# Second attention's front token-major: Newton roots on GpSimd, and VectorE's row operations in other slots

## The reference, cut to what matters

```
q_c = (xh W_DQ) W_UQ            # per head: 512 tokens x 16 features
q_c_norm = q_c * rsqrt(mean(q_c^2) + EPS) * q_norm_w
q_r = q_c_norm W_QR             # 64 more features of the query
kv  = (xh W_DKV) W_UKV;  k_c, v_c = split(kv)
k_c_norm = k_c * rsqrt(mean(k_c^2) + EPS) * k_norm_w
k_r = xh W_KR
scores = ([q_c_norm, q_r] . [k_c_norm, k_r]) * HD**-0.5   # causal softmax, times v_c, times W_O
```

## Time and profile before

| what | value |
|---|---|
| median of 3 runs | 1810.73 us |
| the profiled execution: its own time, its span | 1813.85 us, 1812.1 us |
| second attention (slots with heads) | about 1115 to 1550 us of the span |
| its fronts at work | until about 1490 us |
| granted TensorE clock over the span, mean | 0.966 |

### The profile page before, as it was taken

One profiled execution on the slowest core, in us unless ns is written; L12 is line 12 of the kernel. 1 busy time (PEld: TensorE's weight loads), 2 busy tenths in 40 slices (PEclk: granted clock), 3 DMA queues, 4 the chain that ended last, 5 costly groups with the idle time before them and its releaser, 6 DMA issues. The chain is left out here.

```text
span 1812.1 us, 30114 instructions
## 1 busy us (share of the span) xinstructions
PE 1646.1 (91%) x9124; PEld 1131.0 (62%) x9125; DVE 1204.8 (66%) x4166; ACT 1013.9 (56%) x2528; POOL 550.7 (30%) x683
## 2 busy tenths in 40 slices
PE   6899999999999999978688877899999988899996
PEld 4667676767676767654577645566666664466665
DVE  1797878787878788727444445778888776134245
ACT  1676767676767676624233362566667665652430
POOL 1000101010101010101444288789988763200001
PEclk9999999999999999989799986899999998999998
DMA  4211111111111111120244426888877777000000
GB/s 109 71 30 47 41 47 42 48 42 47 41 48 37 49 39 36 36 93 1 82 136 135 113 64 130 141 141 133 137 131 133 117 123 118 1 6 18 18 24 29
DMA packets 82766, 128.35 MB, mean 71 GB/s; under 512 B 14784, under 2 KB 40848, under 8 KB 82496
## 3 DMA queue, kind: packets, MB, share of 16 engines
q1 hardware_dynamic: 71232, 100.11, 27.1%
q0 software_dynamic: 9664, 25.93, 6.0%
q10 hardware_dynamic: 1728, 0.55, 0.2%
HBM read 73.59 MB, written 35.65 MB: 60 GB/s over the span
## 5 line engine op out<-in xcount | busy, mean ns | idle before, releaser
L413 ACT ACTIVATE c_probs<-c_probs,a_negmax 128x128 f32<-128x128 f32 (+3 forms) x512 | 279.6, 550 | 0.0
L1867 ACT ACTIVATE c_probs<-a_ps_st 128x384 f32<-128x384 f32 (+1 forms) x384 | 189.9, 526 | 134.0 <-PE a_ps_st L1667 129.6
L418 ACT ACTIVATE c_probs<-a_ps_trans 128x512 f32<-128x512 f32 (+1 forms) x256 | 124.7, 487 | 215.0 <-PE a_ps_trans L331 214.0
L2019 DVE CUSTOM_DVE_ANT_0 a_junk<-a_ps_score,c_mask 128x128 f32<-128x128 f32 (+3 forms) x512 | 220.3, 486 | 35.4 <-PE a_ps_score L1645 28.5
L473 DVE CUSTOM_DVE_ANT_0 c_probs<-a_ps_score,c_mask 128x128 f32<-128x128 f32 (+3 forms) x512 | 219.6, 485 | 19.8 <-PE a_ps_score L315 18.7
L536 POOL TENSOR_SCALAR a_rstd<-a_mv 128x4 f32<-128x4 f32 x8 | 1.8, 230 | 705.8 <-DVE a_mv L503 705.8
L331 PE MATMUL a_ps_trans<-c_ident,c_probs 128*128 128x128 f32 x1280 | 188.6, 278 | 17.7 <-DVE c_probs L490 16.1
L331 PEld LDWEIGHTS a_ps_trans<-c_ident,c_probs 128*128 128x128 f32 x1280 | 147.1, 141 | 87.4 <-issue 39.3
L1501 POOL TENSOR_TENSOR a_ms<-a_ms,c_minus_half 128x16 f32<-128x16 f32 x64 | 187.4, 2931 | 1.8 <-DVE a_ms L1988 1.8
L1667 PE MATMUL a_ps_st<-a_qs,a_ks 128*128 128x512 f32 (+3 forms) x512 | 155.4, 365 | 26.4 <-ACT c_probs L1867 14.4
L314 PE MATMUL a_ps_score<-a_kh,a_qs 128*128 128x128 f32 (+3 forms) x512 | 167.4, 351 | 7.0 <-issue 4.6
(11 more groups left out here) (265 smaller groups left out, 3143.4 us busy)
## 6 DMA issues: line engine op xcount, KB each, us to landing
a_qs<-a_qlow SPq DMA_DIRECT2D x128, 128.0 KB, 2.2
bounce<-a_words SPq DMA_DIRECT2D x64, 256.0 KB, 2.0
a_qs<-bounce SPq DMA_DIRECT2D x128, 128.0 KB, 5.7
a_ks<-bounce SPq DMA_DIRECT2D x128, 128.0 KB, 6.3
slot_out<-m_y SPq DMA_DIRECT2D x80, 128.0 KB, 1.7
a_xT<-in_xT SPq DMA_DIRECT2D x8, 512.0 KB
c_X<-in_x SPq DMA_DIRECT2D x8, 512.0 KB
token_rows<-c_X SPq DMA_DIRECT2D x8, 512.0 KB, 5.7
```

The costliest lines, as they stand in the source:

```text
L413: act.activation(at, at, ACT.Exp, scale=-1.0, bias=negmax[:, n % 4, i:i + 1], accum_out=rowsum[:, n % 4, i:i + 1]).then_inc(s_exp, 1)
L418: act.activation(probT[:, n % 4, TGCOL[grp]:TGCOL[grp] + TGLEN[grp]], ps_trans[(3 * n + grp) % 2][:, 0:TGLEN[grp]], ACT.Copy).then_inc(s_p ...
L1867: act.activation(probT[:, r8, col:col + width], ps_st[item % 2][:, 0:width], ACT.Exp).then_inc(s_stc, 1)
L2019: dve.tensor_tensor_reduce(out=junk[:, to:to + keys], in0=ps_score[g][:, at:at + keys], in1=C.mask[:, L - keys:L], scale=-1.0, scalar=3.0e ...
```

## The change

The front's queries and keys are now projected token-major: 128 tokens on the partitions, and for each of 4 token tiles 128 features on the free axis. So a head's 16 features lie side by side, and VectorE sums their squares itself (`tensor_reduce`), GpSimd finds all 64 reciprocal roots of a token row at once (an integer first guess and three Newton steps, 14 small instructions), VectorE multiplies `raw` in place by the roots, broadcast over the 16 features, and TensorE then turns queries (bank `ps_a`) and keys (bank `ps_b`) back to feature-major. The norm weights are applied by ScalarE while it reads the turned banks. `mean8`, `squares`, `widen`, `spread_roots`, `roots` and `s_msc`, `s_wide`, `s_kn` are gone. The feed-forward part's `acc` lies in a new buffer `counts` in place of `roots`, and the first half of `counts` is `fin`.

Steps before and after: `means` 3 and 5, now 3 and 4; roots 4 to 7, now 5 and 6; `normed` 7 and 12, now 8 and 9; turning back to feature-major 7 and 12, now 9 and 11; `high(f, 0)` 8, now 9; `low(f, 0)` 9, now 10; `spread(f, 0)` 10, now 11; `values` 9, now 12; `SG` 11, now 12; `turn` -2, now -1. `rotary` (12), `high(f, 1)`, `low(f, 1)` (13), `spread(f, 1)` (15) and both fills stay.

```diff
-                    if front_at(n, 10) is not None:
-                        spread(front_at(n, 10), 0)
+                    if front_at(n, 11) is not None:
+                        spread(front_at(n, 11), 0)
...
-                def root(f, a, half):
-                    pool.wait_ge(s_msc, f * 2 + a + 1)
-                    at = ms[:, a, 2 * half:2 * half + 2, :].rearrange("p t h -> p (t h)")
-                    pool.tensor_tensor(at, at, C.minus_half[:, 0:2 * HH], ALU.pow).then_inc(s_root, 1)
...
+                def guess_root(f):
+                    pool.wait_ge(s_ms, 2 * f + 2)
                     if f >= 1:
+                        pool.wait_ge(s_nrm, 2 * f)
+                    pool.tensor_scalar(half_mean, half_mean, RMS_EPS / 2, None, ALU.add).then_inc(s_root, 1)
+                    pool.wait_ge(s_root, ROOT_OPS * f + 1)
+                    pool.tensor_scalar(y.bitcast(I32), half_mean.bitcast(I32), -0.5, ROOT_GUESS, ALU.mult, ALU.add
+                                       ).then_inc(s_root, 1)
+
+                def refine_root(f, i):
+                    done = ROOT_OPS * f + 4 * i + 2
+                    pool.wait_ge(s_root, done)
+                    pool.tensor_tensor(xyy, y, y, ALU.mult).then_inc(s_root, 1)
...
+                    pool.tensor_tensor(xyy, xyy, half_mean, ALU.mult).then_inc(s_root, 1)
...
+                    pool.tensor_scalar(xyy, xyy, 1.5, None, ALU.subtract).then_inc(s_root, 1)
...
+                    pool.tensor_tensor(y, y, xyy, ALU.mult).then_inc(s_root, 1)
...
+                    for t in range(TT):
+                        last = pe.matmul(ps_b[:, P * t:P * (t + 1)], xs[f % 2][:, P * t:P * (t + 1)],
+                                         w[:, (SQ, SK)[a], :], start=True, stop=True)
+                    last.then_inc(s_raw, 1)
...
+                def turn_keys(f):
+                    pe.wait_ge(s_nrm, 2 * f + 2)
...
+                        last = pe.transpose(ps_b[:, P * t:P * (t + 1)], raw_k[f % 2][:, P * t:P * (t + 1)], C.ident[:])
+                    last.then_inc(s_bc, 1)
...
+                def weigh(f):
+                    act.wait_ge(s_bc, 2 * f + 2)
...
+                    act.activation(fin, ps_b[:], ACT.Copy, scale=qk_norm[:, 1:2]).then_inc(s_kw, 1)
...
+                    dve.tensor_reduce(ms[:, a, :, :].rearrange("p t h -> p (t h)"),
+                                      sq[:, a, :].rearrange("p (n d) -> p n d", d=HD), AX.X, ALU.add
+                                      ).then_inc(s_ms, 1)
...
+                    dve.wait_ge(s_root, ROOT_OPS * (f + 1))
+                    at = raw(f, a)[:].rearrange("p (t h d) -> p t h d", t=TT, h=HH)
+                    dve.tensor_tensor(at, at, guess[:, a, :, :].unsqueeze(3).to_broadcast([P, TT, HH, HD]),
+                                      ALU.mult).then_inc(s_nrm, 1)
...
+                        dve.scalar_tensor_tensor(words[1][:], ps_a[:], qk_norm[:, 0:1], words[0][:].bitcast(F32),
+                                                 ALU.mult, ALU.subtract).then_inc(s_lo, 1)
```

More of the change, by code:

```diff
@@ L35 @@
 RMS_EPS = 1.1920929e-07
+ROOT_GUESS = float(0x5F3759DF - 0x400000 - 0x80000000)
+ROOT_STEPS = 3
+ROOT_OPS = 4 * ROOT_STEPS + 2
 MASKED = -1.0e30
@@ L96, in layer0_attention @@
         s_xT = S.sem("xT")
-        w, qk_norm, mean8 = folded
+        w, qk_norm = folded
         with ExitStack() as pctx:
@@ L1363, in layer1 @@
         s_turn, s_xs, s_raw, s_rawc, s_sq = (S.sem(n) for n in ("turn", "xs", "raw", "rawc", "sq"))
-        s_ms, s_msc, s_root, s_wide, s_g = (S.sem(n) for n in ("ms", "msc", "root", "wide", "g"))
-        s_bc, s_fin, s_kn, s_hi, s_lo = (S.sem(n) for n in ("bc", "fin", "kn", "hi", "lo"))
+        s_ms, s_root, s_nrm, s_g = (S.sem(n) for n in ("ms", "root", "nrm", "g"))
+        s_bc, s_kw, s_fin, s_hi, s_lo = (S.sem(n) for n in ("bc", "kw", "fin", "hi", "lo"))
         s_v, s_vc = S.sem("v"), S.sem("vc")
@@ L1424, in layer1 @@
         wide = lambda j, i: half[j][:, GL * i:GL * (i + 1)]
-        acc = roots[:].rearrange("p a t d -> p a (t d)")
         FFN = FeedForward(
@@ L1431, in layer1 @@
                  [wide(1, i) for i in range(NF)]],
-            pos=xs, acc=[acc[:, c, :] for c in range(2)],
+            pos=xs, acc=[counts[:, c, :] for c in range(2)],
             ps_turn=[ps_a, ps_b], ps_h=ps_score[0:2], ps_y=[ps_score[2], ps_st[0], ps_st[1]])
@@ L1604, in values @@
                     last.then_inc(s_v, 1)
-                def squares(f, a):
-                    pe.wait_ge(s_sq, f * 2 + a + 1)
-                    if f >= 1:
-                        if a:
-                            pe.wait_ge(s_fin, 2 * f)
-                        else:
-                            pe.wait_ge(s_vc, f)
-                    elif a:
-                        pe.wait_ge(s_msc, 1)
-                    for t in range(TT):
-                        at = (a * TT + t) * HH
-                        last = pe.matmul(ps_a[:, at:at + HH], sq[:, a, P * t:P * (t + 1)],
-                                         mean8[:], start=True, stop=True)
-                    last.then_inc(s_ms, 1)
-                def spread_roots(f, a):
-                    pe.wait_ge(s_wide, f * 2 + a + 1)
-                    if f + 1 < NFRONT:
-                        if a:
-                            pe.wait_ge(s_msc, 2 * f + 3)
-                        else:
-                            pe.wait_ge(s_xs, f + 2)
-                    elif a:
-                        pe.wait_ge(s_vc, f + 1)
-                    else:
-                        pe.wait_ge(s_msc, 2 * f + 2)
-                    for t in range(TT):
-                        last = pe.transpose(ps_a[:, P * t:P * (t + 1)], roots[:, a, t, :], C.ident[:])
-                    last.then_inc(s_bc, 1)
                 def scores(n):
@@ L1828, in square @@
                         act.wait_ge(s_ms, 2 * f - 1 + a)
-                    if a and f >= 1:
-                        act.wait_ge(s_lo, 2 * f - 1)
-                    if not a and f >= 2:
-                        act.wait_ge(s_lo, 2 * f - 2)
-                    act.activation(sq[:, a, :], raw(f, a)[:], ACT.Square).then_inc(s_sq, 1)
+                    act.activation(sq[:, a, :], raw(f, a)[:], ACT.Square, scale=(2 * HD) ** -0.5).then_inc(s_sq, 1)
                 def keep_values(f):
@@ L1893, in _ @@
                         act.activation(yq[:], ps_y[:], ACT.Copy).then_inc(s_yc, 1)
-                    if front_at(n, 8) is not None:
-                        high(front_at(n, 8), 0)
+                    if front_at(n, 9) is not None:
+                        high(front_at(n, 9), 0)
+                    if front_at(n, 11) is not None:
+                        weigh(front_at(n, 11))
                     if front_at(n, 13) is not None:
                         high(front_at(n, 13), 1)
-                    if front_at(n, 9) is not None:
-                        keep_values(front_at(n, 9))
+                    if front_at(n, 12) is not None:
+                        keep_values(front_at(n, 12))
                     if front_at(n, 1) is not None:
@@ L1906, in _ @@
                         square(front_at(n, 3), 1)
-                    if front_at(n, -2) is not None:
-                        features(front_at(n, -2))
+                    if front_at(n, -1) is not None:
+                        features(front_at(n, -1))
                     if n == TURN0 + 1:
@@ L2052, in _ @@
                     if front_at(n, 12) is not None:
-                        normed(front_at(n, 12), 1)
                         rotary(front_at(n, 12))
-                    if front_at(n, 5) is not None:
-                        means(front_at(n, 5), 1)
-                    if front_at(n, 7) is not None:
-                        normed(front_at(n, 7), 0)
+                    if front_at(n, 4) is not None:
+                        means(front_at(n, 4), 1)
+                    if front_at(n, 8) is not None:
+                        normed(front_at(n, 8), 0)
                     if front_at(n, 9) is not None:
-                        low(front_at(n, 9), 0)
+                        normed(front_at(n, 9), 1)
+                    if front_at(n, 10) is not None:
+                        low(front_at(n, 10), 0)
                     if front_at(n, 13) is not None:
@@ L2123, in shape_constants @@
         "lower": rows(P * np.tril(np.ones((E, E)), -1)), "block": heads,
-        "mean8": np.ascontiguousarray(heads[:, ::HD] / f32(HD)),
     }
```

142 lines of the change are left out of this document (72 added, 70 removed).

## The result

The changed kernel takes 1826.38 us (median of 6 runs) beside 1812.24 us of the kernel before on the same chip: a ratio of 1.009, 95% interval 1.0074 to 1.0107, so it is slower by 0.9%. The profiled execution took 1824.94 us with a span of 1823.2 us.

A forecast was written before the change was run, and what follows sets the result against it. GpSimd's root pairs were taken to set the 27.35 us period, the shift's DMA loop the new 26.7: 8 us saved over 12.5 periods, 5 before the heads. 1813.85 - 8 - 5 = 1801, as median 1798 us; range 1770 to 1822.

The forecast's parts named there:

- GpSimd: 14 operations on 64 columns take 4.6 us, 6 with allowance, replacing 11.7 us of powers; its roots leave the chain.
- VectorE's operations: Two reductions at 0.65 us and two multiplications at 0.69 come, old steps go: net +0.9, busy 23.4 us a period.
- TensorE's busy period: `squares` goes, 1.9 us a front, and projections and transposes cost nothing more: from 25.5 to 23.6 us a period.
- VectorE's waits for the front before: VectorE's idle time for turned roots and squares in the kernel before, taken as 3.7 us a front.
- Before the first head: Start of the program: faster roots for the first fronts save 5 us, bounds 0 and 12.
- The loop through `low(f, 0)`, the fill and the shift: From slot 7's exponents to the next slot 7's; sets the new period at 26.7 us, bounds 26.0 and 27.6.
- Fill to landing: Part of the shift's DMA loop, from the start of the fill until the shift lands: 12.9 us.
- to its first mask 0.6 more: Term of the shift's DMA loop: VectorE's slot 0 mask starts 0.6 us after slot 0's scores.
- About a microsecond of remaining waits: Slot 5, where `rotary` waits for `SG` behind `attend` and `values`: about a microsecond on top of VectorE's 23.4 us.
- the engines' 24.6 us: Period if only engines counted: VectorE's 23.4 us and about a microsecond of remaining waits.
- hidden by its own slack: ScalarE's one added copy of 512 columns a front costs nothing; without the slack 0.7 us a period.
- rival B: Gap of 2 to 3 us in slot 7 lowers TensorE's clock in three periods of four: slower, 1820 us; chance 0.24.

The follow-up runs named there:

- best_weigh: Changed kernel with `SG` ahead of `attend`, `values`, `rotary`, `weigh` and square later, `low(f, 0)` ahead of slot 3's mask, shift's DMA issued by ScalarE: 1797.41 us, ratio 0.9935.
- low_early: Changed kernel with VectorE's `low(f, 0)` moved ahead of slot 3's mask: 1803.16 us, ratio 1.0028 to the kernel before.
- weigh_late: Changed kernel with ScalarE's `weigh` and the square beside it moved behind slot 4's last exponentials: 1818.57 us, ratio 1.0049 to the kernel before.
- low_weigh: Changed kernel with `low(f, 0)` ahead of slot 3's mask, and `weigh` and the square behind slot 4's last exponentials: 1806.81 us, ratio 0.9977.
- values_13: Changed kernel with the values' projection one slot later, so `SG` stands directly behind `attend`: 1818.33 us, ratio 1.0112 to the kernel before.
- rot_first_late: Changed kernel with `SG` ahead of `attend`, values in slot 6, `rotary` behind `means(f + 1, 1)`: 1818.36 us, ratio 1.0087 to the kernel before.
- warm: Changed kernel with two extra matmuls, results unread, ahead of slot 7's exponents in each period: 1818.98 us, ratio 1.0106 to the kernel before.
- before_newton: Kernel before with only the roots changed, to three Newton steps on GpSimd, 13 operations each for queries and keys: 1791.06 us, ratio 0.9949.

## Why the prediction was wrong

- **GpSimd: right.** 14 operations of 0.25 to 0.39 us are 0.39 + 0.25 + 3 x 1.32 = 4.6 us, the sum of the forecast. They did not leave VectorE's path altogether (0.6 us of wait in slot 1 of the period shown, 0.3 on average).
- **VectorE's operations: right.** 0.68 us for the reduction (0.65), 0.80 and 0.73 for `normed` (0.69), 0.75 for `low`. TensorE's busy period is 24.1 us in best_weigh, where the clock is 1.00, for 23.6. One reading was off: of the 24.1 us before `means` the row puts 14.2 to `squares` and 9.9 to "issue", so VectorE's waits for the front before were 3.0 us (16.9 + 9.3 + 14.2 over 13.5 fronts), not 3.7.
- **Before the first head: right,** 6 to 8 us for 5.
- **The loop through `low(f, 0)`, the fill and the shift: the right mechanism, mis-sized.** I said 26.7 us, bounds 26.0 and 27.6; the period shown has 28.7. Fill to landing was nearly right (13.3 for 12.9). The term "to its first mask 0.6 more" was 1.0, since VectorE is in `outputs`; the wait for roots, set to nothing, 0.6; each operation some tenths. I had costed the loop as if the engines arrived free at it. low_early shows that the loop was a bound: 11 us for one instruction moved up.
- **"About a microsecond of remaining waits" in slot 5: the step that failed.** It was 3.5 us a front (2.6 where the clock had not fallen in slot 5), and the engines' 24.6 us were never near: with the shift's wait nearly gone the period was still 28.1. I had read off the order that `SG` moved behind `attend` and `values`, and did not walk the chain from `turn_keys` to `rotary` across the three engines.
- **ScalarE's copy "hidden by its own slack": failed too.** Its duration is hidden, its place isn't. `weigh` waits for TensorE ahead of exponentials that TensorE waits for; moving it and the square back gave 0.4 points in weigh_late and 0.5 in low_weigh over low_early.
- **The clock: left out of the sum, and that failed as well.** It is rival B's mechanism, to which I gave 0.24 and 1820 us, with 28.5 us a period; the changed kernel has 29.1 and 1826, so B was nearest. B expected the falls in slot 7 in nine periods of 12. There were three there, and four in slot 5, which no part of the prediction had. The periods with a fall are 2.9 us longer than the others. The Trainium skill, in "TensorE: Matmul & The Clock Gate", section "Why this matters for your kernels", warns of idle gaps between bursts of matmuls. The trace agrees in the direction (0.50 to 0.57 behind waits of 1.0 to 2.2 us), but these gaps are shorter than those that the section names. That the falls follow the two waits is shown by low_early, weigh_late and low_weigh, where each kind of fall goes, or nearly, with its wait.

Two chains of nearly one length, each with a wait behind which the clock falls, explain most of the runs: moving `SG` alone gave nothing (values_13, rot_first_late), repairing the shift's loop alone stopped at 28.1, and both together pass the kernel before. weigh_late doesn't fit the picture of a gap that only moves: it gained 0.6 us a period by itself. Open stays how the loss divides between the chains and the clock: the periods with a fall hold both, and warm could not separate them. What bounds best_weigh at 26.8 and before_newton at 26.5 wasn't tried; their intervals overlap, so which of the two is the faster is open too.

## What to carry to other kernels

When work moves from a slow engine into in-order queues that are 80 to 93% full, sum the new dependences across engines, not the durations: find for each moved step who waits behind it, and walk that chain until it closes. If one repair changes nothing, the wait has moved; try it again together with a repair of the next loop before dropping it. Look at the granted clock period by period: a mean of 0.93 hid that nearly all of the loss stood in seven periods of twelve. And take a many-part change apart: here the arithmetic (Newton steps) gained 0.5% in the old layout, and the rest of the change gave 1.4% away, which came back only with steps put in other places of their queues (0.9935).
